# GpSimd instead of VectorE forms the low parts of the next stage's projection weights in the first feed-forward stage

## What is computed

```python
# x: (8, 256, 256) float32
gate = jax.nn.silu(_qmatmul(x, w_gate, s_gate))   # int8 weights 256 x 1024, one scale per column
up = _qmatmul(x, w_up, s_up)
out = _qmatmul(gate * up, w_down, s_down)         # 1024 x 256
x = _layernorm(x + out)
...
qkv = jnp.einsum('bsh,hf->bsf', x, w_qkv)         # next block: w_qkv is 256 x 6144, float32
```

## Time and profile before

| what | value |
|---|---|
| median of 3 runs | 2550.53 us (2548.64 to 2559.16) |
| profiled execution, its span | 2554.8 us |
| busy share of the span | PE 87%, PE weight load 77%, DVE 66%, ACT 57%, POOL 34% |
| `l0_ffn` in the span | from about 255 to 382 us |

### The profile page before, as it was taken

One profiled execution on the slowest core, in us unless ns is written; L12 is line 12 of the kernel. 1 busy time (PEld: TensorE's weight loads), 2 busy tenths in 40 slices (PEclk: granted clock), 3 DMA queues, 4 the chain that ended last, 5 costly groups with the idle time before them and its releaser, 6 DMA issues. The chain is left out here.

```text
span 2554.8 us, 47770 instructions
## 1 busy us (share of the span) xinstructions
PE 2231.2 (87%) x16471; PEld 1959.9 (77%) x16471; DVE 1673.7 (66%) x4013; ACT 1459.0 (57%) x3819; POOL 862.3 (34%) x887
## 2 busy tenths in 40 slices
PE   6998978999999939999389888899696899996997
PEld 5887868999999929998257666677685576765997
DVE  5776777888888855553388888778464555554554
ACT  4775547777777713333377676776242556563442
POOL 3221110011111130000668787768486243432000
PEclk7788999999999969999689999999798999997999
DMA  4000111000000553332401111000300000000001
GB/s 149 1 1 1 51 50 35 2 18 18 18 18 18 178 157 115 120 103 91 139 38 51 51 51 46 34 28 7 112 8 1 1 1 1 1 1 1 1 1 34
DMA packets 74224, 111.79 MB, mean 44 GB/s; under 512 B 16026, under 2 KB 59666, under 8 KB 72868
## 3 DMA queue, kind: packets, MB, share of 16 engines
q1 hardware_dynamic: 66352, 87.22, 10.7%
q0 software_dynamic: 7488, 21.50, 2.7%
q10 hardware_dynamic: 148, 0.01, 0.0%
HBM read 79.73 MB, written 28.97 MB: 43 GB/s over the span
## 5 line engine op out<-in xcount | busy, mean ns | idle before, releaser
L1909 POOL TENSOR_TENSOR l2a_hb<-l2a_hb,l2a_Cb 128x1024 f32<-128x1024 f32 x128 | 302.8, 2375 | 121.9 <-DVE l2a_hb L2390 121.1
L2390 DVE TENSOR_TENSOR_SCAN l2a_hb<-l2a_dA,l2a_dB 128x1024 f32<-128x1024 f32 x128 | 289.3, 2275 | 72.6 <-PE l2a_dB L1996 30.9
L2231 ACT ACTIVATE l2a_dA<-l2a_delta,l2a_An 128x255 f32<-128x255 f32 x512 | 214.5, 498 | 26.8 <-DVE l2a_delta L2319 13.8
L1996 PE MATMUL l2a_dB<-l2a_diag,l2a_dxT 64*128 64x128 f32 x2048 | 188.4, 305 | 26.8 <-DVE l2a_hb L2390 13.9
L1996 PEld LDWEIGHTS l2a_dB<-l2a_diag,l2a_dxT 64*128 64x128 f32 x2048 | 139.5, 194 | 90.5 <-PE l2a_dB L1996 37.3
L952 PE MATMUL l1a_QK<-l1a_xh,early_wqkv_h 128*128 128x256 f32 x512 | 146.6, 286 | 1.5 <-DVE l1a_xl L128 1.5
L952 PE MATMUL l1a_QK<-l1a_xh,early_wqkv 128*128 128x256 f32 x512 | 144.1, 281 | 0.0
L952 PE MATMUL l1a_QK<-l1a_xl,early_wqkv_h 128*128 128x256 f32 x512 | 143.9, 281 | 0.0
L2016 PE MATMUL l2a_YS<-ident,l2a_hb 128*128 128x128 f32 x1024 | 140.5, 283 | 1.0 <-POOL l2a_hb L1909 1.0
L1211 ACT ACTIVATE l1a_ex<-l1a_S,l1a_nm 128x256 f32<-128x256 f32 x256 | 119.1, 470 | 36.7 <-DVE l1a_nm L1263 36.7
L2016 PEld LDWEIGHTS l2a_YS<-ident,l2a_hb 128*128 128x128 f32 x1024 | 115.0, 144 | 12.1 <-POOL l2a_hb L1909 1.5
(11 more groups left out here) (735 smaller groups left out, 7765.8 us busy)
## 6 DMA issues: line engine op xcount, KB each, us to landing
l2a_Cb<-c_rows SPq DMA_DIRECT2D x8, 2048.0 KB, 7.3
l1f_xl<-moe_x_rows SPq DMA_DIRECT2D x95, 128.0 KB, 2.1
moe_y_rows<-l1f_yo SPq DMA_DIRECT2D x95, 128.0 KB, 1.7
first_raw<-in_L_attn_w_qkv_dram SPq DMA_DIRECT2D x18, 256.0 KB, 2.8
moe_x_rows<-X SPq DMA_DIRECT2D x1, 4224.0 KB, 17.1
l1f_dL<-in_L_ffn_Wd_dram SPq DMA_DIRECT2D x1, 3072.0 KB, 16.8
X<-in_L_attn_x_dram SPq DMA_DIRECT2D x8, 256.0 KB, 5.9
routes_raw<-in_L_attn_w_o_dram SPq DMA_DIRECT2D x4, 512.0 KB, 4.0
```

Of the source, the lines that this page charges most:

```text
L1909: nc.gpsimd.tensor_tensor(h[:, :, :], h[:, :, :], Cb[p][:, s0:s0 + UN, :], ALU.mult).then_inc(hc_ready, 1)
L1996: last = nc.tensor.matmul(out[:, m:m + 2, j * P + a:j * P + a + HP], dxT[q][a:a + HP, j, c * P:(c + 1) * P], diag[q][a:a + HP, j, s0 + m:s ...
L2231: last = nc.scalar.activation(dA[(i * NU + u) % DAS][:, n, 1:SEQ], delta[q][:, c, 1:SEQ], ACT.Exp, scale=An[:, c, s0 + n:s0 + n + 1])
L2390: nc.vector.tensor_tensor_scan(flat(hb[u % RING]), flat(dA[(i * NU + u) % DAS]), dB[u % 2][:, :], 0.0, ALU.mult, ALU.add).then_inc(scanned, 1)
```

## The change

The line that forms a split is taken out of the DVE program and put into the POOL program. POOL's list for one turn of its loop becomes: copy an item for the transpose, splits 0 and 1, `rstd`, splits 2 and 3. ACT, PE and SP are not touched. The semaphore that SP waits for is now raised by POOL.

```diff
         @block.gpsimd
         def _(pool):
-            def item(i, p, first=False):
-                stage(ph, pool, i + 1)
+            def split_low(i, n):
+                m = (i - 2) * SLOTS + n
+                pool.wait_ge(early.high_ready, m + 1)
+                nc.gpsimd.tensor_tensor(low[:, m, :], raw[n][:, :].bitcast(F32), high[:, m, :].bitcast(F32),
+                                        ALU.subtract).then_inc(early.low_ready, 1)
+
+            for i in range(-1, ITEMS + 1):
+                if i + 1 <= ITEMS:
+                    stage(ph, pool, i + 1)
+                if i >= 3:
+                    split_low(i - 1, 0)
+                    split_low(i - 1, 1)
                 if i >= 2:
                     rstd(ph, pool, i - 2)
...
+                if i >= 3:
+                    split_low(i - 1, 2)
+                    split_low(i - 1, 3)
             rstd(ph, pool, ITEMS - 1)
...
                     if step == 7 and not first:
                         normalize(ph, dve, i - 1)
-                    if 5 <= step < 5 + SLOTS and split:
-                        n = i * 4 - 8 + step - 5
-                        dve.wait_ge(early.high_ready, n + 1)
-                        nc.vector.tensor_tensor(low[:, n, :], raw[step - 5][:, :].bitcast(F32), high[:, n, :].bitcast(F32),
-                                                ALU.subtract).then_inc(early.low_ready, 1)
```

## The result

The changed kernel took **2567.43 us** (median; the kernel before beside it 2549.66): a ratio of 1.0060 [1.0043, 1.0076], slower. One of its six runs took 3661.58 us at a granted clock of 0.551; the ratio is that of the other five, whose median is 2566.47. In a second sitting it took 2566.07 against 2552.98, a ratio of 1.0054 [1.0040, 1.0068], +13.1 us. The forecast was 2557, its range 2541 to 2572, with a chance of 0.74 for a change within 0.5% and of 0.21 for slower by over 0.5%; the measured ratios lie just beyond that mark, their intervals on both sides of it. The profiled execution took 2564.65, 1.7 us more than its span.

What follows compares the result with a forecast made beforehand. DVE's loop of work, which the down product on PE waits for, was taken to set the 14.36 us period. Saving 1.78 but losing 2.98 to contention gave +6.6 us in all: 2550.5 + 6.6 = 2557, range 2541 to 2572.

Steps and rivals of the forecast that it cites:

- The loop and the gain: DVE's order from the product of f4 to the low part of f7: losing three splits saves 1.78 us a period.
- rival 3: DVE gets in first nearly always, the period shortens to PE's 12.00 us: -14 us, 2536; chance 0.03.
- POOL's time and the new waits: POOL has time for four subtractions, 5.1 us a period; `rstd` behind splits and SP's load slots cost nothing.
- The contention: DVE and POOL instructions reading SBUF wait for each other: 2.98 us lost a period, +6.6 us in all.
- low part beside split 0: DVE's low part at 320.92 waits for split 0 on POOL and ends later: +0.38 us.
- residual's sum: DVE's residual sum waits for split 1 on POOL: +0.29 us.
- low part of f6: In a race with split 2, DVE's low part waits if POOL is first: +1.07 us.
- normalizations: On DVE, the first waits for split 3, +0.95 us; POOL's copy gets between the two, +0.29 in four items.
- the sentence in brackets: If DVE's low part of f6 starts before split 2, the first normalization waits as long instead.
- The clock: At the down product, PE's clock falls after about 2.2 us idle: 10 to 20 us more, 2567 to 2577; chance 0.22.
- the forecast proper: Contention at about the worked price with at most two clock falls: 2553 to 2563 us, chance 0.54.
- The rule on `rstd`: A skill rule makes DVE wait for `rstd`'s second instruction on POOL, 3 us in all; given a tenth.

Runs made afterwards that it cites:

- e6: Kernel before, with all four splits kept on DVE but placed behind the last low part of the item: 2546.31 us against 2552.98, ratio 0.9976.
- e2: Changed kernel, but POOL subtracts only 8 of each 512 columns, the rest being zero, with the same waits and order: 2542.09 us against 2552.82, ratio 0.9960.
- e7: Kernel before, with splits 1 to 3 on DVE behind the last low part, split 0 on POOL after the residual's sum, POOL's copy held back: 2544.28 us, ratio 0.9967.
- e5: Changed kernel with splits 0 and 1 given back to DVE and splits 2 and 3 left on POOL: 2565.08 us, ratio 1.0049 to the kernel before.
- e8: Changed kernel with two memsets on POOL, which only write, in place of each subtraction: 2549.05 us beside 2555.37, one run.
- e1: Changed kernel with 12 extra unread matmuls filling PE's idle time before the down product, items 3 to 7: ratio 1.0039 to the kernel before.
- e9: Changed kernel with POOL copying the high part, one input, in place of each subtraction: 2546.42 us beside 2555.37, one run.
- e3: Changed kernel with splits 2 and 3 and POOL's copy held until DVE has made the next item's third low part: 2551.96 us, ratio 0.9996.

## Why the prediction was right, and where it was wrong

**The loop and the gain: right.** The period was set by the order of DVE's work from the product of f4 to the low part of f7, and e6 shows it by moving the splits out of this stretch alone. The gain was put at 1.78 us a period; e2 has 1.62 of it. The missing 0.16 to 0.2 is a short wait of DVE for itself, a term that the sum did not have. The product of f7 overwrites the tile that the low part of f5 reads, so it waits until that low part is done (`al_ready`, line 914 of the kernel before). Behind a low part the next instruction starts after 0.33 us where it has nothing to wait for (324.69 to 325.02), but the product of f7 after 0.52 (327.44 to 327.96), with the silu of f7 done at 325.47 already. Before, split 1 stood between the two and covered this. And the floor that the prediction took for PE, 12.00 us of weight loads, is not the one that counts: in e2 and e7 PE's matmuls are busy for 12.3 to 12.4 of 12.7 us and the idle time in front of the down product is down to 0.1, so the period could hardly have become shorter still, and rival 3's 12.00 was out of reach.

**POOL's time and the new waits: right.** "These waits cost nothing": e2 for the semaphores and the order, and the rows of the changed kernel for POOL's queue.

**The contention: right in sum, less so by place.** Of the single prices:

| instruction of DVE | predicted | measured |
|---|---|---|
| low part beside split 0 | +0.38 | +0.42 |
| residual's sum | +0.29 | +0.32 |
| low part of f6 | +1.07 | 0 |
| normalizations | +0.95 and +0.29 | +1.93 |
| low part of f7 | 0 | +0.41 |
| sum | 2.98 | 3.08 |

The low part of f6 was let off, since `rstd`'s second instruction took 0.90 us instead of 0.69 and split 2 came that much later: the low part started at 328.36, split 2 at 328.37. The wait went to the normalizations, as the sentence in brackets in the prediction had it, which met both splits, and the copy then met the low part of f7. That the sum came out within 0.1 us is in part luck: the two low parts were priced the wrong way round, and the normalizations at 1.24 (0.95 and 0.29) instead of 1.93. With DVE's wait for its own low part a period grew by 1.48 at a full clock, against 1.20, and the six by 8.0, against 6.6.

**The clock: the step that failed.** The forecast counted "one or two single falls" at most and gave the mechanism a chance of 0.22, as a rival. It came: four falls, each about 3.4 us long at 0.50 and worth 1.3 to 1.5 us, 5.7 together. The sum without it was +6.6 us, the stage lost 13.7: 8.0 by contention and 5.7 by the clock. The time lies inside the stated range only because the range had been stretched for this rival; the forecast proper, 2553 to 2563, was missed. That 2567.4 also stands at the rival's lower end (2567 to 2577) is in part luck: it had reckoned with 10 to 20 us of clock, and the difference of the first sitting, 17.8, is the larger of the two. The place was named rightly (the down product), the idle time too (about 2.2 expected, 2.4 measured). What was wrong was the weight. The argument against it was that PE is fuller here than around the gap of the third layer; a PE full on both sides did not spare it. Each fall cost less than the least that had been reckoned (1.7 to 3.3). Nor is it the idle time alone that decides, as the rival had it: 2.43 us in front of 299.02 left the clock at 1.00, and in e5 1.75 us went ahead of a fall.

**The rule on `rstd`.** In the kernel before, besides split 1, a low part too began in the midst of `rstd`'s second instruction (324.51 to 325.20) and kept its length:

```profile
324.69 0.41 DVE L921 TENSOR_TENSOR l0f_al<-l0f_a,l0f_ah 128x256 fp32r<-128x256 f32 x1
```

In the changed kernel this POOL instruction ran from 327.51 to 328.41; the low part of f5, begun just before it, took 0.42, and that of f6, begun in its last 0.05 us, 0.41. So these rows stand against the rule for DVE's side of this small instruction. POOL's side is another matter: 0.90 us instead of 0.69, where a low part had begun just before it, here and in e8 (0.89, from 321.90, the low part from 321.82). For the large ones the runs agree with the same section of the Trainium skill (SBUF — State Buffer, Who interferes with whom): it says that a DVE instruction with two SBUF inputs contends with a GpSimd instruction that reads SBUF, and not with one that only writes it, and counts `tensor_scalar` among those that can take both ports. e8 shows both halves: 0.42 and 0.69 unchanged, 2.04 for the normalizations.

## What to carry to other kernels

Before work is moved from DVE to POOL, mark which instructions of DVE run beside it: those with two SBUF operands, and scalings from SBUF to SBUF, will wait for POOL, here for 3.1 us a period where 1.8 were saved. Ask first whether the work can move in time on its own engine, to where that engine waits (e6, -6.7 us), and give POOL only what fits beside statistics and instructions that read PSUM (e7, -8.7 us). And where a change lengthens a stretch in which PE is idle (0.72 to 2.4 us here), price the clock with it: that was 5.7 of the 13.7 us lost, and twelve useless matmuls took it out of the periods (a part came back in the tail).

## What had not been expected of the hardware

- The clock fell at four consecutive down products in the changed kernel and at four in e5, though PE was busy for 13.88 of the 17.31 us from one to the next; the idle time in front was 2.0 to 2.4 us in the one and 1.75 to 2.06 in the other. In neither did it fall behind the first of these idle stretches (2.43 us in front of 299.02, window above; 2.04 in e5). Behind 1.00, 1.08 and 1.37 us (e1, e9, e8) it did not fall in these periods, before the tail. Why the first was spared stays open.
- The two engines seem to take turns by instruction. The pair of normalizations, begun beside split 2, ended 0.15 us behind split 3 (331.35 against 331.20); and POOL waits too: split 2 took 1.56 us instead of 1.27, splits 0 and 1 together 2.74 instead of 2.54. That they alternate is read from these rows and was not tried by itself.
- `normalize` from SBUF to SBUF waits for POOL's writes too, the subtractions of DVE don't.
- A stage made 4.4 us shorter (e3) gave no measurable gain in the whole; in its profiled execution the clock fell once more in the next phase, which is about half of what is missing. The rest was not found.
